# Mixture-of-experts output: a gather of rows that waits by expert in place of by tile

## Chip, cores and metric

The kernel runs on one core of a Trainium2 chip. The metric is the device time of one execution in microseconds, the median of several runs. Shorter is better.

## The reference

All in float32, on x of 32 batches x 32 rows x 1024 columns and a context of 32 x 257 x 1024: a cross-attention, a mixing step within each batch, and a mixture of experts. Only the last is touched:

```python
x = x + cross_attention(layernorm(x), context, Wq, Wk, Wv, Wo)
x = x + mixing(layernorm(x), eta)
x = x + ffn(layernorm(x), gate_w, expert_w)

def ffn(x, gate_w, expert_w):            # x: 1024 rows of 1024, expert_w: 8 x 1024 x 1024
    logits = einsum('bsh,he->bse', x, gate_w)
    topv, topi = top_k(logits, 2)
    w = softmax(topv)
    w_e = einsum('bske,bsk->bse', one_hot(topi, 8), w)
    return einsum('bsh,eho,bse->bso', x, expert_w, w_e)
```

Each row goes to two of eight experts, and its two products are added to it with two weights.

## The kernel before

The program has four stages, one block each: queries, cross-attention, mixing and experts. A block ends with a drain on each engine (the row's line is that of the stage's `with ExitStack`, 834 for mixing, 1263 for experts) and a barrier.

**Plan.** Mixing computes the routing. It writes the rows' numbers and weights into a list in DRAM, slot_scratch, sorted by expert, and the rows after the expert's layernorm into n_scratch. The rows of an expert are cut into tiles of 128, the last of them partly empty (an empty place has a row number out of bounds, which gathers and scatters skip). At its end VectorE makes a plan in `tiles`, an integer tile on one partition (lines 1148 to 1180), each operation waiting for the one before: for each tile its expert (row 0), its number within the expert (1), flags for the split of weights (2, 5, 6), whether the tile is in use (3), and the number of tiles (4). These inputs give 20 tiles. Engines read the plan with `value_load` into registers (the helper `entry`, line 1281; TENSOR_LOAD in the trace).

**Experts (lines 1256 to 1446).** For tile i, with par = i % 2 choosing one of two buffers:
- GpSimd gathers the tile's rows from n_scratch into `xg` (L1323), two tiles ahead.
- TensorE turns them (`turn`, L1423), in the middle of the step of the tile before. ScalarE copies the high part `gT_h` (L1362), VectorE makes the low part `gT_l` (L1387).
- TensorE multiplies by the expert's weights, held as high and low parts, in 48 products (L1441) into two PSUM banks.
- GpSimd gathers what the output holds so far for these rows, `out_x`, into `acc[par]` (L1341). VectorE adds the weighted products to it (L1412, two halves). GpSimd scatters the rows back to `out_x` (L1347).
- Two small loads fetch the row numbers: `idx_out` for the next tile (also the weights of the sum) and `idx` for the tile three ahead (L1318).
- In an expert's first tile ScalarE (L1367) and VectorE (L1393) split half of the next expert's weights, in its second tile the other half; the chunks so freed are loaded again by SyncE (L1299, 512 KB each). In the second tile VectorE's split stands ahead of gT_l.

A row that is in two experts is in two tiles, never twice in one expert. Its second gather must see the first scatter. Before, each gather of acc waits for all earlier scatters, counted on one semaphore, `written`. `wait_apart` (line 98) is a wait followed by an increment of a semaphore `passed` where the value is in a register.

The work is issued in program order on each engine. On GpSimd a step reads: wait for turn(i), gather xg(i+2), wait for the scatters, wait for idx_out, gather acc(i), load idx_out(i+1), wait for xg(i+2), load idx(i+3), wait for the sum of tile i, scatter. All its DMAs are in one queue (q0); SyncE's weight loads are in another (q1). The steps of tiles 0 to 2 are written out, the rest are in a loop with a test whether the tile is in use.

Of the kernel before, what the change touches and what calls it, by code (L numbers as in the profile page):

```python
# [12 lines left out]
ALU = mybir.AluOpType  # L13
# [7 lines left out]
P = 128  # L21
# [31 lines left out]
class Shared:  # L53


    def __init__(self, nc, ctx):
# [10 lines left out]
        self.w = [self.at("w_h", HIGH0, [P, 2 * SLOT], F32R), self.at("w_l", LOW0, [P, 2 * SLOT], F32R)]  # L67
        self.tiles = sb("tiles", [1, 7, COLS], I32)

# [36 lines left out]
def known(t):  # L106
    return isinstance(t, int)
# [720 lines left out]
def mixing(nc, sh, x, eta, gate, expert_w, out, n_dram, slot_dram):  # L828
# [5 lines left out]
    with ExitStack() as ctx:  # L834
# [217 lines left out]
        def _(dve):  # L1052
# [90 lines left out]
            def then(o):  # L1143
                pc[0] += 1
                o.then_inc(plan, 1)
                dve.wait_ge(plan, pc[0])
# [7 lines left out]
            then(dve.tensor_copy(tiles[:, 3, :], f_f[:, 0, :]))  # L1154
            then(dve.tensor_copy(tiles[:, 4, :], first[0:1, E - 1:E].to_broadcast([1, COLS])))
            then(dve.tensor_tensor(first[:, :], first[:, :], n_tiles1[:, :], ALU.subtract))
            first_b = first[0:1, :].unsqueeze(1).to_broadcast([1, COLS, E])
# [7 lines left out]
            then(dve.tensor_copy(tiles[:, 0, :], f_f[:, 0, :]))  # L1165
            then(dve.tensor_copy(tiles[:, 1, :], f_f[:, 1, :]))

            then(dve.memset(only[:, :], 0.0))
# [87 lines left out]
def experts(nc, sh, expert_w, n_dram, slot_dram, out):  # L1256
# [6 lines left out]
    with ExitStack() as ctx:  # L1263
# [6 lines left out]
        idx, xg, idx_loaded, xg_loaded = sh.idx, sh.xg, sh.idx_loaded, sh.xg_loaded  # L1270
        idx_out = sb("idx_out", [P, 2, 2], I32)
        acc = sh.at("acc", STAGE + 8 * D, [P, 2, D])
        t_ps, y_ps = banks[0:2], [banks[2:4], banks[4:6]]

        gT_done, gT_h_ready, gT_l_ready = sem("gT_done"), sem("gT_h_ready"), sem("gT_l_ready")
        idx_out_loaded, acc_loaded, y_done, acc_ready, written = (
            sem("idx_out_loaded"), sem("acc_loaded"), sem("y_done"), sem("acc_ready"), sem("written"))
        passed = sem("passed3")
# [32 lines left out]
        def _(pool):  # L1311
# [18 lines left out]
            load_idx(idx_out, 0, 0).then_inc(idx_out_loaded, 16)  # L1330
            pool.wait_ge(xg_loaded, 32)

            def step(i, par):

                pool.wait_ge(gT_done, 2 * i + 2)
                gather(i + 2, par)

                if not known(i) or i >= 1:
                    wait_apart(pool, written, 16 * i, passed)
                wait_apart(pool, idx_out_loaded, 16 * i + 16, passed)  # L1340
                pool.indirect_dma_start(acc[:, par, :], None, out, bass.IndirectOffsetOnAxis(ap=idx_out[:, par, 0:1], axis=0),  # L1341
                                        bounds_check=B * SQ - 1, oob_is_err=False).then_inc(acc_loaded, 16)
                load_idx(idx_out, i + 1, 1 - par).then_inc(idx_out_loaded, 16)
                pool.wait_ge(xg_loaded, 16 * i + 48)
                load_idx(idx, i + 3, 1 - par).then_inc(idx_loaded, 16)
                wait_apart(pool, acc_ready, 2 * i + 2, passed)
                pool.indirect_dma_start(out, bass.IndirectOffsetOnAxis(ap=idx_out[:, par, 0:1], axis=0), acc[:, par, :], None,  # L1347
                                        bounds_check=B * SQ - 1, oob_is_err=False).then_inc(written, 16)
            steps(pool, step)
            used = pool.value_load(tiles[0:1, 4, 0:1], min_val=E, max_val=MT)  # L1350
            pool.wait_ge(idx_loaded, used * 16 + 48)
            pool.wait_ge(idx_out_loaded, used * 16 + 16)
            pool.wait_ge(written, used * 16)

# [136 lines left out]
```

## Time and profile before

| | |
|---|---|
| median of 3 runs | 1273.03 us (1269.46 to 1277.02) |
| span of the profiled execution | 1263.3 us |
| last stage (experts), first product to end | 979.3 to 1263.3 us |
| TensorE busy over the span | 1126.6 us (89%) |
| VectorE, ScalarE, GpSimd busy | 679.6, 441.1, 259.9 us |
| mean granted TensorE clock | 0.943 of full speed |
| queue q0 (GpSimd's) / q1 (SyncE's and ScalarE's), from 970 us on | 25.22 / 25.17 MB |

The profile is one execution on the chip. Times in it count from the span's start. Busy time of an engine leaves out register, branch, semaphore and DMA-issuing instructions of its sequencer; these have a q behind the engine's name (POOLq is GpSimd's sequencer, SPq is SyncE's). PE is TensorE, DVE is VectorE, ACT is ScalarE, POOL is GpSimd. On POOL an indirect DMA is shown for the time in which its descriptors are made, not until its data has landed. "a <- b" says that a waited until b was done, or in a tile's name that a was written from b. Who released a wait is inferred from semaphore events.

### The profile page before, as it was taken

The page shows a single profiled execution, that of the slowest core. Times are in us where ns is not written, and L with a number is a line of the kernel's source. Part 1 is how long each engine was busy: PE and PEld are TensorE (multiplying, and loading weights), DVE is VectorE, ACT ScalarE, POOL GpSimd, SP SyncE. Part 2 cuts the span into 40 slices and gives each one's busy share as a digit, 9 for nine tenths or more (in the row PEclk, how much of TensorE's full clock was granted, in tenths as well). Part 3 has the DMA queues.
Part 4 walks back from the last instruction along what each step waited for, and adds up shares of the span by engine and source line. Part 5 has one row for each costly group of instructions (what it writes and reads, how often), then busy time and mean ns, then how long its engine had stood idle before and what let it go on. Part 6 is the DMA issues. An engine that isn't in the chain of part 4 may idle for free. (4 is left out here: it accounts for less than half of the span.)

```text
span 1263.3 us, 27032 instructions
## 1 busy us (share of the span) xinstructions
PE 1126.6 (89%) x8474; PEld 994.7 (79%) x8475; DVE 679.6 (54%) x1699; ACT 441.1 (35%) x1111; POOL 259.9 (21%) x436
## 2 busy tenths in 40 slices
PE   6997989999999999999999987999942989989795
PEld 5886889899999999999999965777732867867684
DVE  5442146566666666666666655566675344354441
ACT  3232134444444444444444443111223033323120
POOL 0000211111211111111111101123232323333432
PEclk9999799999999999999999986999965989989898
DMA  7225355465565565565565461543151665566421
GB/s 283 67 109 200 105 169 155 151 198 149 155 198 153 164 184 154 163 184 164 156 182 172 130 218 52 203 84 67 70 164 50 231 222 177 195 212 229 155 97 65
DMA packets 72737, 196.95 MB, mean 156 GB/s; under 512 B 14800, under 2 KB 17232, under 8 KB 68592
## 3 DMA queue, kind: packets, MB, share of 16 engines
q1 hardware_dynamic: 52368, 145.66, 37.1%
q0 software_dynamic: 18016, 42.29, 11.0%
q10 hardware_dynamic: 2304, 8.39, 1.7%
q8 instruction: 26, 0.43, 0.1%
q14 instruction: 23, 0.19, 0.0%
HBM read 159.07 MB, written 44.56 MB: 161 GB/s over the span
## 5 line engine op out<-in xcount | busy, mean ns | idle before, releaser
L593 ACT ACTIVATE prob<-bank,nmax 128x257 f32<-128x257 f32 x256 | 122.2, 478 | 327.1 <-DVE nmax L648 326.8
L648 DVE TENSOR_REDUCE nmax<-bank 128x1 f32<-128x257 f32 x256 | 107.7, 421 | 170.4 <-PE bank L783 170.0
L690 PE MATMUL bank<-cT_h,wkv_h 128*128 128x256 f32 x512 | 157.3, 307 | 0.0
L699 PE MATMUL bank<-wkv_h,cT_h 128*128 128x256 f32 x512 | 154.5, 302 | 0.0
L1441 PE MATMUL bank<-w_h,gT_h 128*128 x320 | 131.4, 411 | 23.6 <-DVE gT_l L1387 23.6
L690 PE MATMUL bank<-cT_h,wkv_l 128*128 128x256 f32 x512 | 145.0, 283 | 0.0
L690 PE MATMUL bank<-cT_l,wkv_h 128*128 128x256 f32 x512 | 144.8, 283 | 0.0
L699 PE MATMUL bank<-wkv_h,cT_l 128*128 128x256 f32 x512 | 144.0, 281 | 0.0
L699 PE MATMUL bank<-wkv_l,cT_h 128*128 128x256 f32 x512 | 144.0, 281 | 0.0
L1441 PE MATMUL bank<-w_h,gT_l 128*128 x320 | 128.5, 401 | 0.0
L1441 PE MATMUL bank<-w_l,gT_h 128*128 x320 | 128.3, 401 | 0.0
L554 POOL DMA_DIRECT2D qcat<-q_scratch x128 | 70.8, 558 | 275.8 <-PE bank L783 271.4
L716 PE MATMUL bank<-ident,prob 128*128 128x128 f32 (+1 forms) x544 | 104.8, 280 | 6.8 <-DVE pT L471 3.8
L623 DVE TENSOR_TENSOR cT_l<-bank,cT_h 128x512 fp32r<-128x512 f32 x128 | 88.4, 692 | 31.3 <-ACT cT_h L564 27.6
L783 PE MATMUL bank<-kcat,qcat 128*128 128x258 f32 x256 | 83.3, 326 | 19.9 <-DMA kcat<-k_scratch 14.7
L690 PEld LDWEIGHTS bank<-cT_h,wkv_h 128*128 128x128 f32 x512 | 97.7, 191 | 0.7
L690 PEld LDWEIGHTS bank<-cT_l,wkv_h 128*128 128x128 f32 x512 | 98.0, 191 | 0.0
L690 PEld LDWEIGHTS bank<-cT_h,wkv_l 128*128 128x128 f32 x512 | 97.3, 190 | 0.0
L699 PEld LDWEIGHTS bank<-wkv_l,cT_h 128*128 128x128 f32 x512 | 97.1, 190 | 0.0
L699 PEld LDWEIGHTS bank<-wkv_h,cT_h 128*128 128x128 f32 x512 | 96.6, 189 | 0.0
L641 DVE TENSOR_SCALAR prob<-prob,rsums 128x257 f32<-128x257 f32 x256 | 91.7, 358 | 9.1
L699 PEld LDWEIGHTS bank<-wkv_h,cT_l 128*128 128x128 f32 x512 | 96.6, 189 | 0.0
(199 smaller groups left out, 2273.1 us busy)
## 6 DMA issues: line engine op xcount, KB each, us to landing
kcat<-k_scratch SPq DMA_DIRECT2D x128, 258.0 KB, 4.2
cx<-in_context SPq DMA_DIRECT2D x32, 1024.0 KB, 5.4
raw<-in_expert_w SPq DMA_DIRECT2D x48, 512.0 KB, 4.1
qcat<-q_scratch POOLq DMA_DIRECT2D x128, 128.0 KB, 5.1
k_scratch<-kT_h SPq DMA_DIRECT2D x32, 258.0 KB, 2.3
k_scratch<-kT_l SPq DMA_DIRECT2D x32, 258.0 KB, 2.5
x_in<-in_x SPq DMA_DIRECT2D x16, 512.0 KB, 4.2
expert_raw<-in_expert_w SPq DMA_DIRECT2D x16, 512.0 KB, 8.1
```

What stands on the lines that cost most here:

```text
L554: pool.dma_start(qcat[c * DH:(c + 1) * DH, par, :, :].rearrange("d (g j) n -> d g (j n)", g=4).bitcast(F32), q_of_batch(b, c // 2)).then_i ...
L593: act.activation(prob[:, 1 - par, s, 0:SK], s_ps[s % 2][:, 0:SK], ACT.Exp, bias=nmax[:, 1 - par, s:s + 1], accum_out=sums[:, 1 - par, s:s ...
L623: dve.tensor_tensor(cT[1][:, par, 2 * m:2 * m + 2, :].rearrange("p a n -> p (a n)"), cT_ps[m % 2][:, :], high, ALU.subtract).then_inc(cT_l ...
L641: dve.tensor_scalar(prob[:, ap, i, 0:SK], prob[:, ap, i, 0:SK], rsums[:, i:i + 1], None, ALU.mult).then_inc(prob_ready, 1)
L648: dve.reduce_max(nmax[:, 1 - par, s:s + 1], s_ps[s % 2][:, 0:SK], AXX, negate=True).then_inc(max_done, 1)
L690: o = pe.matmul(k_ps[:, j * 256:(j + 1) * 256], wkv[x][:, k, j * P:(j + 1) * P], cT[y][:, par, k, :], start=(j == 0 and k == 0 and n == 0) ...
L699: o = pe.matmul(v_ps[:, a * KV:(a + 1) * KV], cT[x][:, par, k, a * P:(a + 1) * P], wkv[y][:, k, KV:2 * KV], start=(a == 0 and k == 0 and n ...
L716: o = pe.transpose(dst[0:rows, n * P:(n + 1) * P], src, ident[:, :])
L783: pe.matmul(s_ps[s % 2][:, 0:SKP], qcat[:, 1 - par, cat_index(s), :], kcat[:, 1 - par, cat_index(s), :], start=True, stop=True).then_inc(s ...
L1441: o = pe.matmul(y_ps[par][h][:, :], gT[a][:, par, k * P:(k + 1) * P], w[b][:, bass.ds(slot + (k * D + h * 512), 512)], start=(k == 0 and n ...
```

## The change

`written` becomes two semaphores, for scatters of even and of odd tiles. The plan gets four rows more: for each tile the count of even and odd tiles that belong to earlier experts (rows 7 and 8), and the counts over all tiles (9 and 10), each times 16 and plus 16. GpSimd reads a tile's two counts and waits for each, then for the scatter of tile i-2, which used the same acc buffer, and then gathers. The wait for the scatter of tile i-1, which used the other idx_out buffer, now stands before the load of idx_out(i+1). Two small loads into an unused tile, `spare`, give each semaphore a first 16, so that no wait is for zero. At the end the two totals are read and waited for.

```diff
-        self.tiles = sb("tiles", [1, 7, COLS], I32)
+        self.tiles = sb("tiles", [1, 11, COLS], I32)
...
+            for p in range(2):
+                then(dve.tensor_scalar(tiles[:, 9 + p, 0:1], first[0:1, E - 1:E], 1.0 - p, None, ALU.add))
+                then(dve.tensor_scalar(tiles[:, 9 + p, 0:1], tiles[:, 9 + p, 0:1], 1, 4, ALU.logical_shift_right, ALU.logical_shift_left))
+                then(dve.tensor_scalar(tiles[:, 9 + p, 0:1], tiles[:, 9 + p, 0:1], 16.0, None, ALU.add))
...
+            for p in range(2):
+                then(dve.tensor_scalar(tiles[:, 7 + p, :], e_f[:, 1, :], 1.0 - p, None, ALU.add))
+                then(dve.tensor_scalar(tiles[:, 7 + p, :], tiles[:, 7 + p, :], 1, 4, ALU.logical_shift_right, ALU.logical_shift_left))
+                then(dve.tensor_scalar(tiles[:, 7 + p, :], tiles[:, 7 + p, :], 16.0, None, ALU.add))
...
+        spare = sb("spare", [P, 2, 2], I32)
...
-        idx_out_loaded, acc_loaded, y_done, acc_ready, written = (
-            sem("idx_out_loaded"), sem("acc_loaded"), sem("y_done"), sem("acc_ready"), sem("written"))
+        idx_out_loaded, acc_loaded, y_done, acc_ready = (
+            sem("idx_out_loaded"), sem("acc_loaded"), sem("y_done"), sem("acc_ready"))
+        written = [sem("written0"), sem("written1")]
...
             pool.wait_ge(xg_loaded, 32)
+            for p in range(2):
+                pool.dma_start(spare[:, p, :], slot_dram[0:P, :]).then_inc(written[p], 16)
 
             def step(i, par):
 
                 pool.wait_ge(gT_done, 2 * i + 2)
                 gather(i + 2, par)
 
-                if not known(i) or i >= 1:
-                    wait_apart(pool, written, 16 * i, passed)
+                for p in range(2):
+                    earlier_experts = pool.value_load(tiles[0:1, 7 + p, bass.ds(i, 1)], min_val=16, max_val=16 * MT)
+                    wait_apart(pool, written[p], earlier_experts, passed)
+                wait_apart(pool, written[par], 8 * (i - par) + 16, passed)
                 wait_apart(pool, idx_out_loaded, 16 * i + 16, passed)
                 pool.indirect_dma_start(acc[:, par, :], None, out, bass.IndirectOffsetOnAxis(ap=idx_out[:, par, 0:1], axis=0),
                                         bounds_check=B * SQ - 1, oob_is_err=False).then_inc(acc_loaded, 16)
+                if not known(i) or i >= 1:
+                    wait_apart(pool, written[1 - par], 8 * (i + par) + 16, passed)
                 load_idx(idx_out, i + 1, 1 - par).then_inc(idx_out_loaded, 16)
...
                 pool.indirect_dma_start(out, bass.IndirectOffsetOnAxis(ap=idx_out[:, par, 0:1], axis=0), acc[:, par, :], None,
-                                        bounds_check=B * SQ - 1, oob_is_err=False).then_inc(written, 16)
+                                        bounds_check=B * SQ - 1, oob_is_err=False).then_inc(written[par], 16)
             steps(pool, step)
             used = pool.value_load(tiles[0:1, 4, 0:1], min_val=E, max_val=MT)
+            every_scatter = [pool.value_load(tiles[0:1, 9 + p, 0:1], min_val=16, max_val=16 * MT) for p in range(2)]
             pool.wait_ge(idx_loaded, used * 16 + 48)
             pool.wait_ge(idx_out_loaded, used * 16 + 16)
-            pool.wait_ge(written, used * 16)
+            for p in range(2):
+                pool.wait_ge(written[p], every_scatter[p])
```

## Rows read from the trace of the kernel before

**Rows 1.** Waits by engine and line: who waited for whom, total us, times, longest.

```profile
DVE acc L1412 <- DMA acc<-out_x,idx_out: 95.3, 17, 8.1
PE bank L1441 <- DVE gT_l L1387: 23.6, 6, 7.7
```

**Rows 2.** Timeline of VectorE and TensorE: start, duration, engine, line, [idle before <- releaser].

```profile
990.13 6.89 DVE L825 TENSOR_TENSOR w_l<-expert_raw,w_h 128x1024 fp32r<-128x1024 f32 x6
...
1174.13 1.28 DVE L1387 TENSOR_TENSOR gT_l<-bank,gT_h 128x512 fp32r<-128x512 f32 x2
...
1175.73 0.79 PE L1441 MATMUL bank<-w_h,gT_h 128*128 x1 [7.68 <-DVE gT_l L1387]
```

**Rows 3.** Timeline of GpSimd, experts (same columns; descriptors made, not landed).

```profile
986.07 1.04 POOL L1323 DMA_INDIRECT xg<-n_scratch,idx  x1 [1.44 <-DMA idx_out<-slot_scratch]
...
1000.55 1.06 POOL L1323 DMA_INDIRECT xg<-n_scratch,idx  x1 [0.30 <-issue]
1005.20 1.00 POOL L1341 DMA_INDIRECT acc<-out_x,idx_out  x1 [3.59 <-DMA out_x<-acc,idx_out]
...
1013.78 1.06 POOL L1323 DMA_INDIRECT xg<-n_scratch,idx  x1 [0.30 <-issue]
...
1044.61 1.05 POOL L1323 DMA_INDIRECT xg<-n_scratch,idx  x1 [0.49 <-issue]
1047.52 0.99 POOL L1341 DMA_INDIRECT acc<-out_x,idx_out  x1 [1.86 <-issue]
1049.29 0.58 POOL L1318 DMA_DIRECT2D idx_out<-slot_scratch  x1 [0.78 <-issue]
...
1056.27 1.05 POOL L1323 DMA_INDIRECT xg<-n_scratch,idx  x1 [0.80 <-issue]
...
1129.10 1.00 POOL L1341 DMA_INDIRECT acc<-out_x,idx_out  x1 [1.74 <-issue]
...
1154.87 1.05 POOL L1323 DMA_INDIRECT xg<-n_scratch,idx  x1 [0.49 <-issue]
```

**Rows 4.** Chain that ended last: start, us (a DMA's from issue to landing).

```profile
1016.58 8.61 DMA acc<-out_x,idx_out
...
1043.08 3.40 DMA out_x<-acc,idx_out
...
1047.52 4.23 DMA acc<-out_x,idx_out
...
1058.68 6.68 DMA acc<-out_x,idx_out
...
1157.72 8.26 DMA acc<-out_x,idx_out
```

**Rows 5.** Busy time by stretch (tile 3); last columns: PE clock, DMA share, GB/s.

```profile
1032.00:1041.00 9.00, 6.86 (x18) 5.44 (x19) 2.12 (x4) 0.00 (x0) 2.67 (x3) 0.62 0.81 300
```

**Rows 6.** Timeline of SyncE: weight loads issued in tiles 2, 5 and 10.

```profile
1015.91 3.71 SPq L1299 DMA_DIRECT2D raw<-in_expert_w  x4
...
1059.02 3.70 SPq L1299 DMA_DIRECT2D raw<-in_expert_w  x4
...
1129.38 3.74 SPq L1299 DMA_DIRECT2D raw<-in_expert_w  x4
```

**Rows 7.** Timeline of VectorE: the plan's last operation.

```profile
967.81 0.17 DVE L1180 CAST tiles<-only 1x26 int32<-1x26 f32 x1
```

**Rows 8.** Line 834, end of mixing: ns min/median/max, first and last start us.

```profile
L834 DVEq DRAIN  x1: 2397/2397/2397, 968.0 to 968.0; - x1
L834 POOLq DRAIN  x1: 5465/5465/5465, 969.9 to 969.9; - x1
```

**Rows 9.** Lines 1350 and 1263, end of experts on GpSimd's sequencer (same columns).

```profile
L1350 POOLq TENSOR_LOAD <-tiles x1: 293/293/293, 1253.6 to 1253.6; - x1
...
L1263 POOLq DRAIN  x1: 8562/8562/8562, 1254.5 to 1254.5; - x1
```

**Rows 10.** Line 1318 in the first steps (980 to 990 us): landing of index loads.

```profile
DMA to landing us min/median/max: 1.9/3.5/5.2
```

## The prediction

> **What bounds the kernel now.** I read the waits first, by engine. In the expert stage TensorE is idle for 23.6 us before its products, always for the low half of a turned tile, gT_l, which VectorE makes; VectorE itself waits 95.3 us in 17 tiles for gathered output rows, acc [rows 1]. So the first question is what holds a gather, not what the products cost. The order of VectorE's work then shows how the one becomes the other: after the sum of tile 12 it splits four weight chunks and only then makes gT_l of tile 14 (start 1174.13, 1.28 long); TensorE resumes at 1175.73 after 7.68 us of idling and then runs without a gap to its last tile [rows 2]. The pattern of weight splits tells the experts' first tiles: 0, 2, 5, 8, 10, 12, 15 and one of the last. Nothing after tile 12 delays the end, since from there TensorE is the bound. What the change gains or loses is therefore its sum over the gathers of tiles 1 to 12, plus what it adds at the stage's two ends.
>
> Next I read GpSimd's list. In each tile it issues the scatter of tile i-1, the gather xg for tile i+2, the gather acc for tile i, and two loads of indices. The chain shows a scatter landing after 3.40 us (tile 3's), and the gather of tile 4, issued 1047.52, landing after 4.23 [rows 3, 4]. Where weights are being loaded the gather needs 8.61 (tile 2) or 8.26 (tile 12) [rows 4]. In such a tile the DMA engines are 0.81 busy over 9 us at 300 GB/s [rows 5]. A landing there can better be counted from the start of xg: 1016.58 + 8.61 less 1013.78 is 11.4 us, 1157.72 + 8.26 less 1154.87 is 11.1 [rows 3, 4]; these are the first and last of seven loaded tiles (2, 3, 6, 8, 9, 11, 12), of which the others lie at 10.8 to 11.3, mean 11.1. It hardly matters there when acc was issued. The tile whose gather starts just ahead of the weights, tile 5, lands earlier (6.68 after issue).
>
> **The gathers of non-first tiles (1, 3, 4, 6, 7, 9, 11).** The wait for scatter i-1 goes. It is worth less than a scatter: xg and its descriptors stand between anyway. Tile 4 has its scatter (tile 3's) at 1043.08, landed 1046.48, xg at 1044.61, acc at 1047.52: the gather starts 2.91 after xg, some 1.0 after the landing [rows 3, 4]. In exchange GpSimd's sequencer now reads two counts from SBUF and passes three waits more. What two reads cost is seen in the next step: from the start of acc at 1047.52 to the load of idx_out at 1049.29 it is 1.77 us, with two reads, a product and the DMA's dispatch in it [rows 3]. A single read in the closing lines begins at 1253.6 and the drain behind it begins at 1254.5 [rows 9], which allows some 0.6 for one. With 0.15 (an estimate, from the gaps around the waits in these starts) for each of four waits and increments, acc starts 1.77 + 0.6 = 2.4 after xg. The gain is 2.9 - 2.4 = 0.5 us for tile 4 and, as the next like it, at most 0.5 for tile 7 (I take 0.25). Note that xg + 2.4 is 1047.0 in tile 4, still after the scatter's landing at 1046.48: the overlap that the change permits is not reached; only the wake-up behind the wait is saved.
>
> Tile 1 is the one with a real wait: xg 1000.55, acc 1005.20 [rows 3], 4.65 apart. The gather could start 2.2 us sooner. But xg is queued behind that scatter and acc behind xg; so I take 0.4 and keep 0 and 2.2 as ends. In the loaded tiles 3, 6, 9 and 11 landing follows xg, whose issue does not move: 0, with 1.75 as the other end for each (below). Sum: -0.5 - 0.25 - 0.4 = -1.15 us.
>
> A rule speaks against the change here. [rows 4, 5] show landings that follow the load and not the issue. The Trainium skill, "DMA: Bandwidth & Descriptors", section "Queues, rings and completion order", says that each DMA engine takes a ring's descriptors in order and turns between queues packet by packet. By its first half an earlier acc only queues behind xg, which would leave tile 1 at 0 and the sum at -0.75; that agrees with the seven loaded tiles. By its second half an earlier gather would share with weight transfers sooner; that would be the faster rival.
>
> **First tiles (2, 5, 8, 10, 12).** They must still wait for every earlier scatter. The waits stand in the order even count, odd count, with a read between. Where tile i-1 is odd (2, 8, 10, 12), both reads are over when it lands, and about 0.2 is added behind it (one more wait); in tiles 2, 8 and 12 the load hides it (0), in tile 10 I count 0.2. Tile 5 waits for tile 4, an even one: the odd count is read only after the landing, 0.6 + 0.15 + 0.15 = 0.9 us later. Its gather starts at 1058.68, the first weights at 1059.02 [rows 4, 6]; with 0.9 more it is 0.6 behind them, as tile 2 is (1015.91 against 1016.58). Then it lands at xg + 11.1 = 1056.27 + 11.1 = 1067.4 in place of 1058.68 + 6.68 = 1065.4 [rows 3, 4]: +2.0, the lower end 0.9. Tile 15 is late in the same manner, where TensorE has slack: 0. Sum: +2.2.
>
> The load of idx_out now waits for the scatter in place of the gather. By the starts above that has landed, so it costs 0. Queued behind it are only the index loads; their cover is xg's lead of two tiles.
>
> **The plan.** VectorE gets 12 operations more. The last one there took 0.17 us, and at 0.2 from start to start twelve take 2.5 [rows 7]. They end the mixing stage on VectorE, but GpSimd's drain ends it: 969.9 + 5.47 = 975.4, against 968.0 + 2.40 = 970.4 for VectorE's [rows 8]. 2.5 of 5.0 us of cover: 0. Without the cover it would be 2.5.
>
> **The two spare loads.** They stand ahead of the first steps, and tile 0's gather, now right behind the xg at 986.07 [rows 3], has to wait until they have landed. Small loads there take 1.9 to 5.2 us to land [rows 10]; issued at 985.6 and 986.2 (an estimate: the first takes the place of that xg, the second follows 0.6 later) they let it start at 989.1 to 992.4. With tile 4's 4.23 it lands at 993.4 to 996.6. VectorE is in its splits until 990.13 + 6.89 = 997.0 [rows 2]: 0. With a loaded landing up to 4 us late instead.
>
> **The end.** Two more reads stand between the last scatter and GpSimd's drain, which begins at 1254.5 and takes 8.56 us to the end [rows 9]. The scatter has landed by then. 2 x 0.6 = 1.2 us, or 0 if the drain ends by something that does not move. I take 1.2, since no row shows such a thing.
>
> **Sum.** -1.15 + 2.2 + 0 + 0 + 1.2 = +2.25 us. The profiled execution has a span of 1263.3; it would be 1265.6. The median shown, 1273.0, is 9.7 above the span (the three runs 6.2 to 13.7), which I carry over: 1275.3.
>
> **Rivals.** (a) Slower: a first tile's gather, issued 0.2 to 0.9 later, falls behind one weight transfer more. The four transfers are issued within 3.70 us [rows 6], 1.1 apart, so such a delay often crosses one; at tile 5 it decides from 0.34, and at tile 10, where gather and weights start at 1129.10 and 1129.38 [rows 3, 6], from 0.28. Price: 0.52 MB at 300 GB/s [rows 5] is 1.75 us, in each of five first tiles 8.7; with -1.15 and +1.2 this is +8.8: 1281.8. Tiles 2 and 12 speak against it, both fully behind the weights and no later than the rest. (b) Faster: the gathers of tiles 3, 6, 9 and 11 start 0.3 to 0.5 earlier and get ahead of the fourth transfer, 4 x 1.75 = 7.0; with all of tile 1's 2.2, 0.75 for tiles 4 and 7, 1.1 lost in the first tiles and 1.2 at the end it is -7.7: 1265.3. Tile 5's early landing speaks for it, the constant 11.1 against it. Should it hold, TensorE's idling of 7.68 us before tile 14 is the most that remains to be gained. (c) It does nothing: reads and wake-up cancel in all tiles and the drain hides the end: within 1 us of 1273.
>
> **How the numbers follow.** Forecast 0.42, (c) 0.29, (a) 0.16, (b) 0.13. The first two lie within 0.5% (6.4 us, about what a measurement of this kernel can tell from no change), (a) and (b) beyond it: faster 0.13, same 0.71, slower 0.16. The range leaves out the outer halves of (a) and (b) and takes in half of the runs' own spread: 1266.5 to 1281.5.
>
> **What would show it.** Right: in non-first tiles acc starts 2.3 to 2.5 us after xg and after the scatter's landing; loaded tiles land 11 us after xg as before; tile 5 lands about 2 us later against tile 4's sum; TensorE's idle time before its products stays at 22 to 26 us; GpSimd's drain is still the last at the end of the mixing stage. Wrong: acc less than 2 us after xg, or loaded non-first tiles landing at 9.5 us (then it is b); first tiles landing at 12.5 and more (then a); tile 0's sum not at VectorE's first opportunity; the drain of GpSimd no longer the last.

## The result and the profile after

| | before | changed |
|---|---|---|
| median | 1271.72 us (1267.33 to 1277.02, 6 runs) | 1280.88 us (1277.90 to 1287.19, 6 runs) |
| ratio | 1 | 1.0076, 95% interval 1.0047 to 1.0104 |
| profiled execution, span | 1263.3 us | 1276.3 us |

The changed kernel is slower, by 9.2 us in these runs; a second comparison (e11 below) gave 1.0050 (1.0027 to 1.0072), 5.0 us between the medians and 6.4 by the ratio. The forecast was 2.25 us.

The two profiles differ by 13.0 us. TensorE turns the first tile of the expert stage at 975.69 us before and at 982.23 after, so 6.5 of the 13.0 lie ahead of that stage. They can't be laid to the change: in the profiles of all the kernels below this point lies anywhere from 977.7 to 989.3 us, and the profiled execution before is the earliest of all. The rest is read within the stage, counted from its first turn.

| from the first turn, us | before | changed |
|---|---|---|
| sum of tile 0 starts | 21.2 | 22.2 |
| of tile 1 | 34.5 | 34.1 |
| of tile 4 | 76.4 | 76.3 |
| of tile 5 | 90.0 | 91.6 |
| of tile 9 | 146.7 | 148.5 |
| of tile 10 | 159.1 | 163.0 |
| of tile 12 | 190.6 | 194.3 |
| products of tile 14 start | 200.0 | 203.7 |
| last product ends | 273.0 | 278.0 |
| end of the span | 287.6 | 294.1 |

In this pair of profiles the stage is 6.5 us longer, in three parts: 3.7 in the ring of gathers and sums up to tile 12 (a tile's gather waits for earlier scatters, its scatter for its sum, and the sum for the gather), 1.3 between the products of tile 14 and the last, where TensorE runs without a gap, and 1.5 behind them.

One profile is one execution, and the executions of one kernel differ by nearly as much as this. The experiments below leave more profiles with either order of waits, and they are the measure of how much one pair can say. The products of e1 and e11 run at the changed kernel's rate, those of e3, e2, e4 and e5 at that of before.

| us | waits | tile 1's step | tile 5's | tile 10's | tiles 2 to 12 | behind the last product | stage |
|---|---|---|---|---|---|---|---|
| before | before | 13.2 | 13.6 | 12.4 | 156.1 | 14.7 | 287.6 |
| e1 | before | 14.8 | 15.0 | 15.7 | 157.3 | 14.9 | 290.4 |
| e3 | before | 13.4 | 12.3 | 15.8 | 157.3 | 14.8 | 289.7 |
| changed | changed | 11.9 | 15.3 | 14.5 | 160.3 | 16.1 | 294.1 |
| e11, the same kernel | changed | 12.0 | 16.3 | 12.1 | 156.6 | 15.5 | 289.6 |
| e2 | changed | 10.8 | 15.7 | 15.0 | 160.0 | 17.0 | 295.6 |
| e4 | changed | 12.4 | 14.8 | 16.1 | 160.1 | 15.7 | 293.3 |
| e5 | changed | 13.5 | 15.9 | 15.4 | 160.0 | 15.5 | 292.8 |

A step is the time from the sum of the tile before to that of the tile. The stage has a mean of 289.2 us in the three with the waits of before and of 293.1 in the five others, and one of the five, e11, lies among the three.

The waits of the changed kernel (who waited for whom, total us, times, longest) answer to [rows 1]:

```profile
DVE acc L1430 <- DMA acc<-out_x,idx_out: 100.1, 18, 7.6
PE bank L1459 <- DVE gT_l L1405: 21.9, 6, 5.3
```

VectorE's wait for gathered rows did not shrink: 100.1 us here against 95.3. Nor did it clearly grow, since it is 85.2 in e11 and 91.2 and 92.0 in e1 and e3. GpSimd's timeline shows the single steps (start, duration, what; [idle before <- releaser]), for tiles 0, 1, 4, 5 and 10, to be held against [rows 3]:

```profile
991.81 1.08 POOL L1343 DMA_DIRECT2D spare<-slot_scratch  x2 [0.66 <-DMA xg<-n_scratch,idx]
993.20 1.06 POOL L1333 DMA_INDIRECT xg<-n_scratch,idx  x1 [0.30 <-issue]
999.41 1.48 POOL L1355 DMA_INDIRECT acc<-out_x,idx_out  x1 [5.15 <-DMA spare<-slot_scratch]
...
1008.28 1.05 POOL L1333 DMA_INDIRECT xg<-n_scratch,idx  x1 [0.50 <-issue]
1010.88 1.00 POOL L1355 DMA_INDIRECT acc<-out_x,idx_out  x1 [1.56 <-issue]
...
1050.93 1.05 POOL L1333 DMA_INDIRECT xg<-n_scratch,idx  x1 [0.50 <-issue]
1053.74 0.99 POOL L1355 DMA_INDIRECT acc<-out_x,idx_out  x1 [1.75 <-DMA out_x<-acc,idx_out]
...
1062.82 1.05 POOL L1333 DMA_INDIRECT xg<-n_scratch,idx  x1 [0.93 <-PE bank L1441]
1066.01 1.43 POOL L1355 DMA_INDIRECT acc<-out_x,idx_out  x1 [2.14 <-issue]
...
1134.59 1.05 POOL L1333 DMA_INDIRECT xg<-n_scratch,idx  x1 [0.51 <-issue]
1137.53 0.99 POOL L1355 DMA_INDIRECT acc<-out_x,idx_out  x1 [1.88 <-issue]
```

Tile 0's gather starts 6.2 us after xg, behind the landing of the spare loads; it was 1.35. Tile 1's starts 2.6 us after xg in place of 4.65. Tile 4's starts 2.81 after, where it was 2.91: nothing worth the name. Tile 5's, which waits for an even tile, starts 3.19 after xg in place of 2.4. Tile 10's starts 2.94 after, and SyncE had begun to load weights at 1136.70:

```profile
1136.70 13.51 SPq L1309 DMA_DIRECT2D raw<-in_expert_w  x5
```

Before, that gather was 0.28 us ahead of the weights [rows 3, 6]; now it is 0.8 behind, and takes 7.38 us to land where 5.3 had been enough (the sum of tile 10 begins at 1134.78, 5.7 us after the gather's issue). In the chain (start, us from issue to landing) tiles 5 and 10 now look more like the other loaded tiles, and TensorE's products take 11.20 us per tile, in every tile of the last stretch (10.90 to 10.93 in the same view of before):

```profile
1066.01 7.48 DMA acc<-out_x,idx_out
...
1137.53 7.38 DMA acc<-out_x,idx_out
...
1194.23 11.20 PE bank L1459 x48
...
1254.61 5.63 PE bank L1459 x24
```

No product, operand shape or order was changed. That was in no part of the prediction, and the first experiments ask for it.

That a first tile's gather fell behind the weights is not the change alone. In the eight profiles of the table and that of e9 there are 45 gathers of tiles 2, 5, 8, 10 and 12. Eight were issued 0.28 us or more ahead of the first weight load and landed in 4.2 to 6.7 us; the other 37 landed in 6.8 to 9.0. Tile 10 is ahead by that much in one of the three profiles with the waits of before (in e3 it starts with the first load, within 0.01 us, and lands in 8.9; in e1 it is 1.2 behind) and in one of the five others, e11: the changed kernel itself, whose gather is 0.36 ahead, lands in 4.94 us and brings the step to 12.1 us. (e11 has a second such landing in tile 2, whose step is 11.3 us where the other profiles of the table have 14.3 to 15.3; with these two its stage is the shortest of the five.) Tile 5 is ahead by that much in two of the three and in none of the five (0.14 in e2, where it lands in 7.8).

### The profile page after: what moved, and what is told of

Its sections match the earlier page's. It is cut to its first block and busy times, and to the rows that moved or that the text cites. A ratio compares the mean times of both kernels' runs of the same rounds, so it can differ in the third digit from the quotient of the medians.

```text
span 1276.3 us, 27273 instructions
## 1 busy us (share of the span) xinstructions
PE 1138.9 (89%) x8474; PEld 997.4 (78%) x8475; DVE 681.3 (53%) x1711; ACT 440.6 (35%) x1111; POOL 260.2 (20%) x438
## 3 DMA queue, kind: packets, MB, share of 16 engines
q0 software_dynamic: 18080, 42.30, 11.3%
## 5 line engine op out<-in xcount | busy, mean ns | idle before, releaser
L783 PE MATMUL bank<-kcat,qcat 128*128 128x258 f32 x256 | 83.9, 328 | 20.7 <-DMA kcat<-k_scratch 14.8
L1380 ACT ACTIVATE gT_h<-bank 128x512 fp32r<-128x512 f32 x42 | 22.9, 595 | 217.0 <-PE bank L1441 206.0
```

Of the source, the lines that this page charges most:

```text
L783: pe.matmul(s_ps[s % 2][:, 0:SKP], qcat[:, 1 - par, cat_index(s), :], kcat[:, 1 - par, cat_index(s), :], start=True, stop=True).then_inc(s ...
L1380: act.activation(gT[0][:, par, h * 512:(h + 1) * 512], t_ps[h][:, :], ACT.Copy).then_inc(gT_h_ready, 1)
```

## Experiments

e1 to e4 ran on one chip, e5 to e8 on a second, e9 to e11 on a third and e12 on that of the first, each beside the kernel before. Ratios are to the kernel before on the same chip, with their 95% intervals; where kernels ran on different chips, the ratios are what can be compared.

### Layout: e1 and e2

The plan tile has eleven rows in place of seven. That moves every buffer allocated behind it by 416 bytes: gT_h starts at byte 198016 of a partition before (a multiple of 64) and at 198432 after (a multiple of 32 only). e1 has the new size and nothing else of the change:

```diff
-        self.tiles = sb("tiles", [1, 7, COLS], I32)
+        self.tiles = sb("tiles", [1, 11, COLS], I32)
```

> The kernel before with nothing changed but the size of the plan tile in SBUF, 11 rows in place of 7; the four new rows are never written or read. All buffers behind it lie 416 bytes further, as they do in the changed kernel, and so no longer on a multiple of 64 bytes. Theory L (layout): the changed kernel's products take 11.20 us per 48 where before took 10.93, in every tile, though no product was changed, and its earlier stages are late by some us too; if the addresses are the reason, this run shows 11.2 us per 48 products and is 3 to 7 us slower than before. Theory W (waits and reads): the loss is all in GpSimd's list and the faster products of before are a matter of the chip or the run; then this is within 2 us of before, with 10.9 us per 48.

Measured: 1278.90 us against 1276.33, 1.0013 (0.9992 to 1.0033). The chain of its last stretch:

```profile
1196.76 11.20 PE bank L1441 x48
1207.97 0.87 PE bank L1423 x8
1208.84 11.21 PE bank L1441 x48
```

e2 is the changed kernel with a row more, which brings gT_h to 198528, again a multiple of 64:

```diff
-        self.tiles = sb("tiles", [1, 11, COLS], I32)
+        self.tiles = sb("tiles", [1, 12, COLS], I32)
```

> The changed kernel with one unused row more in the plan tile (12), which brings all buffers behind it back to a multiple of 64 bytes. Theory L: 10.93 us per 48 products again, and 3 to 7 us less than the changed kernel, that is 2 to 6 us above before. Theory W: nothing moves, 9 us above before.

Measured: 1280.26 us, 1.0037 (1.0017 to 1.0057). Its products:

```profile
1197.06 10.90 PE bank L1459 x48
1207.97 0.87 PE bank L1441 x8
1208.84 10.93 PE bank L1459 x48
```

So the place of the buffers sets the rate of the products: from turn to turn a tile of the last stretch takes 12.08 us with the buffers at the one place (changed, e1, e11) and 11.78 at the other (before, e2 to e5), with either kernel's code. What makes the products slower there (the stationary operand gT's address is the one that moved; the weights w did not) was not taken apart. For the whole run it is worth less than expected: e1's interval, -1.0 to +4.2 us, takes in zero and the 1.3 us read from the profile, and leaves out most of the 3 to 7 that I expected. The ring bounds most of the stage and takes up the slower products. And e2 stays 4.7 us above before without the layout's share: the larger part of the loss is elsewhere.

### The plan alone: e3

The kernel before with the twelve new operations, which nobody reads (diff: the two blocks of `then(...)` from the change).

> The kernel before with the twelve new operations of the plan and a plan tile of 12 rows (buffers on multiples of 64 bytes); nobody reads the new rows, and the waits are those of before. Prediction: VectorE ends the mixing stage 2.5 us later, GpSimd's drain still ends last, 0 us (within 1 of before). Rival: the end of the stage moves by up to 2.5 us, since the changed kernel's mixing stage was 2.7 us longer in its profile.

Measured: 1275.87 us, 0.9996 (0.9974 to 1.0017). No cost of the operations shows; the interval allows 2.2 us. The drains at the end of its mixing stage show the cover, to be held against [rows 8]:

```profile
L834 DVEq DRAIN  x1: 2401/2401/2401, 973.5 to 973.5; - x1
L834 POOLq DRAIN  x1: 5505/5505/5505, 974.3 to 974.3; - x1
```

VectorE's drain ends at 975.9, GpSimd's at 979.8.

### The order of the two reads: e4

```diff
-                for p in range(2):
-                    earlier_experts = pool.value_load(tiles[0:1, 7 + p, bass.ds(i, 1)], min_val=16, max_val=16 * MT)
-                    wait_apart(pool, written[p], earlier_experts, passed)
+                earlier = [pool.value_load(tiles[0:1, 7 + p, bass.ds(i, 1)], min_val=16, max_val=16 * MT) for p in range(2)]
+                for p in range(2):
+                    wait_apart(pool, written[p], earlier[p], passed)
```

> As e2_aligned, but both counts are read before either is waited for, so that after the landing of an even scatter no read follows. If the late read is what costs tiles 5 and 10 their place ahead of the weight loads, tile 5 gains 0.6 us at its gather's issue and up to 2 at its landing: 1 to 3 us faster than e2_aligned. If the plain length of the list (two reads and three waits between xg and acc) is the cost, it is within 1 us of e2_aligned.

Measured: 1280.05 us, 1.0035 (1.0011 to 1.0059), the same as e2 on the same chip. In its profile tile 5's gather does start 0.6 sooner after xg (2.57 us in place of 3.20) and its sum follows tile 4's by 14.8 us, not 15.7; but the run isn't faster. A read behind the landing of an even scatter is not the main cost.

### The spare loads: e5

From e2, with the two lines of the spare loads moved up, behind the first load of idx:

```diff
             load_idx(idx, 1, 1).then_inc(idx_loaded, 16)
+            for p in range(2):
+                pool.dma_start(spare[:, p, :], slot_dram[0:P, :]).then_inc(written[p], 16)
             pool.wait_ge(xg_loaded, 16)
```

> As e2_aligned (the changed kernel with buffers on multiples of 64 bytes), but the two spare loads are issued right behind the first load of idx, in which GpSimd waits 2.3 us anyway, and not behind the gather of tile 1. If their late landing cost the stage its start (tile 0's gather was issued 6.2 us after xg in place of 1.4, and its sum came 1.0 to 3.9 us later), the gather of tile 0 comes at once, its sum lies at 21 us from the first turn, and the run is 1 to 3 us faster than e2_aligned. If the ring of later tiles takes up such a start, it is within 1 us of it.

Measured: 1283.09 us, 1.0055 (1.0036 to 1.0074). Tile 0's gather now starts 1.9 us after xg (5.6 in e2, 6.2 in the changed kernel), and tile 0's sum lies 20.7 us from the first turn (25.1 in e2), the last scatter 279.2 (282.0). The times don't follow: this ran on another chip than e2, and the intervals of the two overlap. So the late landing costs tile 0 its start, and up to 2.8 us of one profile's stage, but no gain in time was shown.

e2, e4 and e5 show in passing the overlap that the weaker wait allows. In tile 1 both counts have been read by the time xg starts, and the gather starts 1.36 us after xg and 2.7 after the scatter of tile 0, which before and in e3 it waited for. It gains nothing there in e5 (13.5 us from sum to sum, as before), where weight loads stand beside it and it lands only after 8.48 us.

### Two reads more: e8

From e5, with each count read and waited for twice:

```diff
-                for p in range(2):
+                for p in (0, 0, 1, 1):
                     earlier_experts = pool.value_load(tiles[0:1, 7 + p, bass.ds(i, 1)], min_val=16, max_val=16 * MT)
```

> As e5_spare_early, with each of the two counts read and waited for twice: two reads and two waits more in each tile ahead of the gather of acc, which should start 1.3 to 1.5 us later after xg. If an issue delay passes on into the ring of tiles 1 to 12, it costs 12 times 1.3, some 12 to 16 us. If landings in loaded tiles go by the load (11 us after xg whatever the issue), only the unloaded tiles 1, 4, 7 and the first tiles 5 and 10 lose: 3 to 7 us.

Measured: 1298.32 us, 1.0171 (1.0148 to 1.0193), 15.2 us above e5 on the same chip. In the loop the gathers of non-first tiles start 4.2 us after xg (2.8 to 3.0 in e5). The sums, from one tile's to the next, show where that goes:

| us from the sum before, tile | 2 | 3 | 4 | 5 | 6 | 7 | 8 | 9 | 10 | 11 | 12 |
|---|---|---|---|---|---|---|---|---|---|---|---|
| before | 15.0 | 15.5 | 11.4 | 13.6 | 15.1 | 11.2 | 15.1 | 15.4 | 12.4 | 16.2 | 15.3 |
| changed | 15.3 | 15.4 | 11.5 | 15.3 | 15.4 | 11.7 | 14.5 | 15.3 | 14.5 | 16.0 | 15.3 |
| e5 | 14.7 | 15.5 | 11.1 | 15.9 | 15.1 | 11.6 | 14.5 | 15.7 | 15.4 | 15.8 | 14.7 |
| e8 | 15.5 | 15.5 | 12.8 | 16.3 | 15.5 | 12.8 | 16.1 | 15.5 | 16.1 | 16.0 | 16.5 |
| e9 (below) | 15.2 | 15.2 | 9.8 | 12.9 | 15.8 | 10.2 | 15.9 | 14.4 | 13.0 | 16.6 | 14.9 |

The loaded non-first tiles 3, 6, 9 and 11 take 1.3 to 1.4 us of delay at the issue and lose at most 0.4: there the landing does go by the load. The unloaded tiles 4 and 7 lose all of it (1.7 and 1.2), the first tiles 0.4 to 1.8. And with the unloaded ring over 12 us a tile, the last six tiles, bound by TensorE before, are bound by it too: from the sum of tile 13 to that of 19 e8 takes 76.3 us, e5 67.1. The count of tiles that pay was wrong in my narrower figure, and its mechanism right in four of the eleven.

### The reads hidden: e9

From e5; the next tile's counts are read ahead of the wait for the sum, and kept in registers:

```diff
+            counts = [pool.alloc_register(f"count{p}") for p in range(2)]
+            bound = pool.alloc_register("bound")
+
+            def read_counts(i):
+                for p in range(2):
+                    pool.reg_load(counts[p], tiles[0:1, 7 + p, bass.ds(i, 1)])
+            read_counts(0)
+
+            def at_least(sem, count):
+                pool.reg_alu(bound, count, 16, ALU.max)
+                wait_apart(pool, sem, pool.snap(bound), passed)
...
                 for p in range(2):
-                    earlier_experts = pool.value_load(tiles[0:1, 7 + p, bass.ds(i, 1)], min_val=16, max_val=16 * MT)
-                    wait_apart(pool, written[p], earlier_experts, passed)
+                    at_least(written[p], counts[p])
...
+                read_counts(i + 1)
                 wait_apart(pool, acc_ready, 2 * i + 2, passed)
```

> As e5_spare_early, but tile i+1's two counts are read at the end of step i, ahead of the wait for the sum of tile i, where GpSimd idles 1 to 6 us, and kept in registers. Only the waits stand between xg and acc. If the reads are the cost of the changed list: a non-first tile's gather starts 1.9 to 2.2 us after xg (2.9 in e5), the last scatter lies 2 to 4 us nearer to the first turn than in e5 (279.2), and the run is at before or 1 to 2 us under it. If the reads are not the cost, it stays with e5, 7 us above before.

Measured: 1274.77 us against 1276.76, 0.9982 (0.9963 to 1.0001); the changed kernel itself on the same chip (e11) 1.0050. Tile 4's step in its timeline:

```profile
1055.65 1.04 POOL L1375 DMA_INDIRECT out_x<-acc,idx_out  x1 [5.16 <-DVE acc L1442]
1057.17 1.05 POOL L1333 DMA_INDIRECT xg<-n_scratch,idx  x1 [0.48 <-issue]
1058.53 1.00 POOL L1366 DMA_INDIRECT acc<-out_x,idx_out  x1 [0.30 <-issue]
```

The gather starts 1.36 us after xg and 2.9 after the scatter, before a scatter's 3.4 us are over. This is the overlap that the weaker wait allows, now in the loop too: tiles 4 and 7 take 9.8 and 10.2 us, and tiles 5 and 10, once more ahead of the weights, 12.9 and 13.0. The last scatter lies 273.1 us from the first turn; e5 has 279.2. e5 differs from e9 in the place of the reads alone: 1.0055 (1.0036 to 1.0074) against 0.9982 is 9.3 us, on two chips. Against e11 on the same chip it is 7.0 us between the medians, of which the layout and the spare loads can be a part. Both say that the two reads ahead of the gather cost more than the wait that they replaced. Against before the gain is 2 us, and the interval just reaches no gain (1.0001).

### The order of the gathers: e6 and e7

e6 is from e5, e7 from the kernel before (buffers as in e2). Both only move two lines:

```diff
-                pool.wait_ge(gT_done, 2 * i + 2)
-                gather(i + 2, par)
...
                                         bounds_check=B * SQ - 1, oob_is_err=False).then_inc(acc_loaded, 16)
+                pool.wait_ge(gT_done, 2 * i + 2)
+                gather(i + 2, par)
```

> As e5_spare_early, with the gather of acc(i) ahead of the gather of xg(i+2) in GpSimd's step. Theory Q (queue): what makes a gather of acc land 11 us after xg in tiles with weight loads is that it stands behind xg in one queue, and that xg, two reads and the waits stand ahead of its issue; only with acc first does the removal of the wait give anything. Then a non-first tile's gather starts about 2.5 us after its scatter and lands within 8 us of it, the sums of tiles 1 to 12 lie 12 us apart in place of 14.3, TensorE's waits for gT_l fall from 22 us to under 8, and the run is 10 to 20 us faster than before. Theory B (bandwidth): a burst of xg, acc, scatter and four weight transfers takes its 12 us in any order; then acc lands at most 2 us sooner and the run is within 5 us of before.

> The kernel before (one semaphore, wait for every scatter), with only the order of the two gathers turned as in e6 and the buffers on multiples of 64 bytes. Theory Q: the gather of acc(i) still starts 4.2 us after the scatter, but nothing is queued ahead of it; 8 to 16 us faster than before. e6 less e7 then is what the change is worth where it can act: e6 faster by up to 5 us if waiting for scatter i-1 matters, equal or slower if it does not. Theory B: within 5 us of before. Rival: xg, now behind the wait for the scatter, comes 3 us later and delays the turn of tile i+2; then TensorE waits in its transposes.

Measured: e6 1293.85 us, 1.0132 (1.0111 to 1.0154); e7 1304.28 us, 1.0235 (1.0203 to 1.0268). Both are slower, against both theories; the rival named for e7 is what came. e6's waits:

```profile
DVE acc L1429 <- DMA acc<-out_x,idx_out: 115.1, 17, 8.5
PE bank L1440 <- DMA xg<-n_scratch,idx: 29.9, 14, 5.0
PE bank L1458 <- DVE gT_l L1404: 5.9, 5, 2.4
```

TensorE's wait for gT_l mostly goes, as theory Q had it, and a new one takes its place: the turns now wait 29.9 us for xg (31.5 in e7; 0.3 at most in the kernels so far). Nor does acc land sooner for standing ahead of xg. In tile 3 its gather starts at 1045.76 and the sum at 1054.09, 8.3 us later, as long as in the loaded tiles of before:

```profile
1042.67 2.06 POOL L1362 DMA_INDIRECT out_x<-acc,idx_out  x1 [0.31 <-issue]
1045.76 1.26 POOL L1352 DMA_INDIRECT acc<-out_x,idx_out  x1 [1.03 <-issue]
1047.32 1.00 POOL L1333 DMA_INDIRECT xg<-n_scratch,idx  x1 [0.30 <-issue]
1051.81 0.58 POOL L1328 DMA_DIRECT2D idx_out<-slot_scratch  x1 [3.49 <-issue]
1058.27 0.57 POOL L1328 DMA_DIRECT2D idx<-slot_scratch  x1 [5.88 <-issue]
1059.17 1.04 POOL L1362 DMA_INDIRECT out_x<-acc,idx_out  x1 [0.32 <-issue]
```

There a scatter was issued 3.1 us ahead of the gather. In the first tiles of e7, where every scatter has landed and xg comes 1.4 to 2.3 us later, it is 7.6 to 8.5 us from gather to sum all the same.

The rows show the second loss too. The load of idx waits for xg, and the scatter stands behind that load: the sum of tile 3 was done at 1055.5, its scatter is issued at 1059.17. e6 is faster than e7 on one chip, by 10 us between the medians and 13 by the ratios: where scatter and gather stand next to each other, the weaker wait is worth that much, its reads paid.

### A gather one step earlier: e10, and e12

e10 is the kernel before with one more idea: the rows of a non-first tile are gathered at the end of the step before, ahead of the wait for the sum. The first tile's gather stays where it was. One semaphore is enough, since the expert's first tile has waited for all earlier experts.

```diff
-                if not known(i) or i >= 1:
-                    wait_apart(pool, written, 16 * i, passed)
-                wait_apart(pool, idx_out_loaded, 16 * i + 16, passed)
-                pool.indirect_dma_start(acc[:, par, :], None, out, ...)
+                if known(i) and i == 0:
+                    gather_acc(0, 0)
+                else:
+                    number = entry(pool, i, 1, COLS - E)
+                    wait_apart(pool, written, 16 * i, passed)
+                    with pool.If(number < 1):
+                        gather_acc(i, par)
...
+                following = entry(pool, i + 1, 1, COLS - E)
+                with pool.If(following > 0):
+                    gather_acc(i + 1, 1 - par)
                 wait_apart(pool, acc_ready, 2 * i + 2, passed)
```

> From the kernel before, with its single semaphore and a wait for all scatters up to tile i-1 at its old place; but where the plan says that tile i+1 is not the first of its expert, its rows are gathered at the end of step i, before GpSimd waits for the sum of tile i, and so before scatter i is even issued. Buffers on multiples of 64 bytes. The theory: what the weaker order could give lies in the gather's place in GpSimd's list, which the change left as it was. Then sums of non-first tiles wait for products alone, VectorE's waits for gathered rows fall from some 95 us to under 50, TensorE's waits for gT_l from 22 to under 8 us, and the run is 10 to 22 us faster than before. Rival (bandwidth): these gathers now run beside the same weight loads and starve xg or each other; then within 5 us of before.

Measured: 1271.00 us, 0.9964 (0.9935 to 0.9994): faster, by 4.6 us, at the rival's size. (The edit also waits at the end for the one gather that is issued for the tile after the last.) Its waits:

```profile
DVE acc L1423 <- DMA acc<-out_x,idx_out: 31.1, 7, 8.2
PE bank L1452 <- DVE gT_l L1398: 17.4, 5, 6.1
```

VectorE's waits fall as forecast, TensorE's hardly. e12 turns one thing more, in VectorE's step: gT_l of the next tile ahead of the second half of the weight split.

```diff
-                for half, what in ((1, 5), (0, 2), (1, 6)):
-                    if what == 2:
-                        rows_low(i + 1, 1 - par)
-                        if known(i) and i == 0:
-                            for c in range(2, KC):
-                                split_low(dve, sh, 1, c)
+                rows_low(i + 1, 1 - par)
+                if known(i) and i == 0:
+                    for c in range(2, KC):
+                        split_low(dve, sh, 1, c)
+                for half, what in ((1, 5), (0, 2), (1, 6)):
```

> As e10_gather_early, and in VectorE's step the low half gT_l of the next tile stands ahead of the second half of the weight split, not behind it. In e10 VectorE waits only 31 us for gathered rows, yet TensorE still waits 17.4 us for gT_l in five places; theory: each of these is the first tile's sum, late by its scatter and gather, plus the four splits (4.6 us) that stand before gT_l. Then TensorE's waits fall to under 5 us, and the run is 6 to 14 us faster than e10, 10 to 19 us faster than before. Rival: the splits now come later, in the second half of the tile, and the weights of the next expert with them; TensorE then waits for w_l at an expert's first tile what it gained: within 3 us of e10.

Measured: 1261.38 us against 1275.12, 0.9893 (0.9856 to 0.9931): 13.7 us faster than before, the best of all. TensorE's waits for gT_l are down to 2.4 us in all; the largest now is for xg:

```profile
PE bank L1433 <- DMA xg<-n_scratch,idx: 10.4, 4, 3.0
```

So the order of VectorE's splits and gT_l made most of the five stalls, as expected. e12's order on VectorE was not tried without e10's gathers, so how the 13.7 us divide between the two is known only through e10's 4.6.

### The changed kernel again: e11

> The changed kernel itself, once more, beside e9 and e10 on one chip, for the size of its loss: 0.5 to 1.0% over before, 12.08 us per tile of products.

Measured: 1281.74 us against 1276.76, 1.0050 (1.0027 to 1.0072), with 12.08 us per tile of products.

## Why the prediction was right, and where not

Its range held the time (1280.88 in 1266.5 to 1281.5), and most of its chance lay on no change; what came was a loss of 0.76% and, measured again, 0.50%, on the border between its forecast and its rival (a), to which it had given 0.16. That the range held owes something to luck: it held by 0.6 us, e11 with 1281.74 would have been outside it, and two costs that the profiles show, dearer reads in the loop and the layout, were not in the sum.

**What bounds the stage**: right. Sums up to tile 12 carry the loss, and the stall before tile 14 passes it on.

**Gathers of non-first tiles**: the step that failed. "acc starts 1.77 + 0.6 = 2.4 after xg" holds only for the steps written out (2.6 and 2.5 in tiles 1 and 2). In the loop it is 2.8 to 3.0 in non-first tiles, against 2.3 to 2.9 before. The term that was too small is the reads. I had priced them where GpSimd makes no descriptors, 0.29 us in the trace for the load itself [rows 9]; in the changed kernel they stand beside those of xg (all 40 of them, ns min/median/max):

```profile
L1351 POOLq TENSOR_LOAD <-tiles x40: 286/473/960, 992.9 to 1253.9; - x40
```

In tile 4 the two loads take 0.47 and 0.58 us, in tile 7 0.91 and 0.29: 0.5 to 0.6 more than two of 0.29, which is what lies between 2.4 and 2.8 to 3.0. The waits and increments cost 0.17 each, as taken. So the gain of 0.5 in tile 4 was none (11.3 to 11.4 with the waits of before, 11.1 to 11.5 with those of the change), and tile 7 lost 0.5 (11.2 to 11.7, and 11.6 to 11.7 in e4, e5 and e11; only e2 has 11.2). Only tile 1 gained, and more than I took: from sum to sum 13.2 became 11.9, 1.3 us of the 2.2. The queue ahead of it, by which I had cut that to 0.4, did not hold it; e6 and e7 show the same from the other side. The in-order half of the rule that I had quoted from the Trainium skill (DMA: Bandwidth & Descriptors, Queues, rings and completion order) is thus no ground for the constant 11 us of loaded tiles; e8 supports the load itself, for the non-first ones.

**First tiles**: tile 5 as forecast, +1.7 for +2.0, and the other profiles bear it out (12.3 to 15.0 us with the waits of before, 14.8 to 16.3 with the others). Tile 10 got 0.2 in the sum and cost 2.1 in this pair, which looks like rival (a) at the place that it named. It isn't shown to be the change: its gather starts only 0.15 later after xg, while the weights came 1.1 us earlier against it, and over all profiles its step is 12.4, 15.7 and 15.8 us with the waits of before and 14.5, 12.1, 15.0, 16.1 and 15.4 with the others. Its early landing in the profile of before was one outcome of a close race, and the margin of 0.28 us that I read there was that execution's. Tiles 2, 8 and 12 stayed, and no first tile landed 12.5 us after xg, the sign that I had given for (a). The forecast had the mechanism (ahead of the weights or behind them) and took it for fixed.

**Plan**: right, 0 (e3). **Spare loads**: forecast 0 with up to 4 as the end. The gather waited 5.15 us for them and started later than my latest, 6.2 after xg (5.1 in e11); tile 0's sum was 1.0 us late (22.2 for 21.2; 21.3 in e11), and tile 1's gain took that up.

**The end**: +1.2 forecast, 1.5 measured, and in part of other things. From the last scatter's issue to GpSimd's drain it is 4.7 us in place of 4.0 (4.0 to 4.3 in the three profiles with the waits of before, 4.7 in all five others), and the drain takes 8.72 in place of 8.56 [rows 9], 0.8 together, where I had 1.2. The rest is tile 19's gather, which lands only 0.2 us before the last product ends, so that both halves of its sum come behind that product, the second 0.8 us behind it in place of 0.15; this part lies anywhere from 0.15 to 1.7 in the five profiles.

**Not in the prediction**: the layout. It slows products by 2.5% in every tile; where TensorE is the bound, from tile 14 on, it costs the 1.3 us (73 to 74 us from the products of tile 14 to the last at the one place, 74 to 75 at the other). In the run as a whole e1 could not tell it from nothing.

Open: what part of the 9.2 or 6.4 us is whose. The stage's 6.5 us are divided up in one pair of profiles, and the second profile of the changed kernel has none of its 2.1 us in tile 10; of times, e2 puts at least 2.2 us on the change without the layout. Shown is that the reads ahead of the gather cost it: with them twice (e8) the kernel is 15 us slower still, and with them off the path (e9) the loss is gone. That a gain takes its place is not.

## What to carry to other kernels

A wait is worth what it delays beyond the instructions around it: before weakening one, lay the removed wait beside the register reads and computed waits that the finer rule needs, and put those where the engine idles anyway. If the weaker order is to give something, move the freed operation as well; here the same freedom, used one step earlier and with VectorE's order mended, was worth 13.7 us in place of a loss. After adding rows to a small tile, look at the start addresses of the large ones behind it. And before a margin of a few tenths of a microsecond in one profile carries an argument, look at the same place in a second profile of the same kernel: here the same gather won its race in one and lost it in the other.

## What the runs showed of the hardware

- TensorE's float32r products of 128x512 run at 10.93 us per 48 with the stationary tile gT at 198016 or 198528 bytes, and at 11.20 with it at 198432, under the same granted clock (1.00) and in both kernels' code. Which operand's address matters, and whether 64 bytes is the step, was not tried.
- A pair of register reads with their waits on GpSimd's sequencer costs 1.3 us of issue time (e8, where the second pair waits for counts that the first has already found reached). The load within a read takes 0.29 us by itself and up to 0.96 beside or just behind the start of a gather (changed kernel, line 1351).
- In a tile with four weight loads a gather of 512 KB lands some 8 us after its issue, ahead of xg in its queue or behind it (7.6 to 8.5 from issue to sum in the first tiles of e7, 7.1 to 9.0 to the landing in most others); without the loads in 3.7 to 4.4 in tiles 4 and 7. Where it was issued 0.28 us or more ahead of the first load, it landed in 4.2 to 6.7.
